# A decoder layer on one core: a new order and new lags for the attention stage, its norm factors on ScalarE, and the weights split later

## What is computed

```python
q, k, v = (x @ W.T for W in (Wq, Wk, Wv))             # 16 heads of 8
att = einsum('nqhd,nkhd->nhqk', q, k)                 # the heads of one token attend to each other
out = einsum('nhqk,nkhd->nqhd', softmax(att / sqrt(8)), v).reshape(N, S, D)
x = layernorm(x + out @ Wo.T + bo)
scores = einsum('bhsd,bhtd->bhst', xpos(x), xpos(ctx, downscale=True)) * decay_mask
x = layernorm(x + einsum('bhst,bhtd->bhsd', scores, ctx))       # retention, no softmax
w, chosen = top_k(x @ gate, 2)                        # 2 of 8 experts, softmax over the two
eo = einsum('ebsi,eih->ebsh', silu(x @ w1) * (x @ w3), w2)
x = layernorm(x + einsum('ebsh,bse->bsh', eo, tok_w))
# layernorm(x) = (x - mean) / sqrt(var + 1e-5), over the 128 features
```

## Time and profile before

| what | us |
|---|---|
| median of the three runs | 1015.34 |
| lowest and highest run | 1014.36, 1017.56 |
| the profiled execution, first to last instruction (span) | 1027.0 |
| first to last copy of q and v (ScalarE), 32 duos | 23.1 to 500.0 |
| first expert matmul | 652.3 |
| busy: TensorE, VectorE, ScalarE, GpSimd | 839.8, 794.7, 607.7, 654.8 |

### The profile page before, as it was taken

One profiled execution on the slowest core, in us unless ns is written; L12 is line 12 of the kernel. 1 busy time (PEld: TensorE's weight loads), 2 busy tenths in 40 slices (PEclk: granted clock), 3 DMA queues, 4 the chain that ended last, 5 costly groups with the idle time before them and its releaser, 6 DMA issues.

```text
span 1027.0 us, 35115 instructions
## 1 busy us (share of the span) xinstructions
PE 839.8 (82%) x12164; PEld 639.6 (62%) x12164; DVE 794.7 (77%) x2219; ACT 607.7 (59%) x1416; POOL 654.8 (64%) x738
## 2 busy tenths in 40 slices
PE   1667699999999999989979770699999999999600
PEld 1445466666666666656655440599899999999500
DVE  4787899998988989878856642588888888888575
ACT  1123457667667777666766851466666666666355
POOL 0338776699989999988997456044444444444443
PEclk9687899999999999999998965799999999999855
DMA  9312122122232231212222002222222222222186
GB/s 307 79 27 48 35 52 54 36 66 67 47 72 52 65 68 50 65 37 60 47 50 63 23 22 63 66 64 61 61 63 65 65 62 64 63 61 59 45 257 222
DMA packets 145303, 72.72 MB, mean 71 GB/s; under 512 B 75024, under 2 KB 134544, under 8 KB 145136
## 3 DMA queue, kind: packets, MB, share of 16 engines
q1 hardware_dynamic: 124800, 40.56, 17.1%
q0 software_dynamic: 8640, 17.84, 5.2%
q10 hardware_dynamic: 11696, 12.08, 3.6%
HBM read 42.11 MB, written 28.34 MB: 69 GB/s over the span
## 4 chain that ended last, share of the span: by engine, by line
PE 33%; POOL 28%; issue 11%; DVE 3%; DMA 2%; another core or an unknown queue 1%; ACT 1%; POOLq 0%; SPq 0%; DVEq 0%; ACTq 0%
POOL prod_ev L1551 14%; POOL routed_rows L1568 9%; PE QKV L773 9%; PE ST L773 9%; PE XT L801 5%; PE SC L801 5%; POOL rs L1531 3%; DMA prod_ev<-token_halves 1%; DMA routed_rows<-xe,pos 1%; PE YY L589 1%; POOL frs L1613 1%; PE YY L791 1%; PE TR L791 1%; PE SC L562 1%
## 5 line engine op out<-in xcount | busy, mean ns | idle before, releaser
L1551 POOL TENSOR_TENSOR prod_ev<-e_sb,q_v 128x512 f32<-128x512 f32 x256 | 300.3, 1206 | 77.5 <-PE YY L589 40.1
L1600 POOL DMA_INDIRECT token_halves<-w_new,tok_i x142 | 137.9, 971 | 32.5 <-issue 22.2
L1568 POOL DMA_INDIRECT routed_rows<-xe,pos x128 | 131.2, 1025 | 30.4 <-issue 30.0
L1151 DVE TENSOR_TENSOR prod_qk<-q_v,QKV 128x2048 f32<-128x2048 f32 x64 | 145.4, 2274 | 4.9 <-ACT q_v L870 4.9
L1453 DVE TENSOR_TENSOR prod_ev<-prod_qk,prod_ev 128x1024 f16<-128x1024 f32 x71 | 87.0, 1225 | 56.1 <-ACT prod_ev L1028 31.1
L773 PE MATMUL QKV<-k_t,w_hl 128*128 128x256 f16 x852 | 117.2, 274 | 0.0
L773 PE MATMUL ST<-k_t,w_hl 128*128 128x256 f16 x852 | 116.9, 274 | 0.0
L411 POOL TENSOR_TENSOR marks<-half_c 128x1 f32<-128x1 f32 x103 | 19.7, 192 | 149.7 <-DVE w_new L1469 149.1
L1037 ACT ACTIVATE prod_qk<-QKV,silu_scale 128x512 f32<-128x512 f32 x142 | 90.0, 683 | 41.3 <-PE QKV L773 41.3
L1028 ACT CAST prod_ev<-prod_qk 128x1024 f16<-128x1024 f32 x71 | 74.2, 1045 | 62.9 <-DVE prod_qk L1479 62.9
L1479 DVE SCALAR_TENSOR_TENSOR prod_qk<-ST,hid_scale,prod_qk 128x512 f32<-128x512 f32 x142 | 99.5, 742 | 2.9 <-PE ST L773 1.8
(11 more groups left out here) (171 smaller groups left out, 1785.9 us busy)
## 6 DMA issues: line engine op xcount, KB each, us to landing
w_new<-routed_rows SPq DMA_DIRECT2D x71, 130.0 KB
prod_ev<-token_halves SPq DMA_DIRECT2D x16, 512.0 KB, 4.9
x_sb<-x SPq DMA_DIRECT2D x32, 128.0 KB, 2.8
x_res<-x SPq DMA_DIRECT2D x128, 32.0 KB
head_rows<-o_n SPq DMA_DIRECT2D x32, 128.0 KB
o_t<-head_rows SPq DMA_DIRECT2D x64, 64.0 KB
ctx_sb<-ctx SPq DMA_DIRECT2D x32, 128.0 KB
out<-prod_qk ACTq DMA_DIRECT2D x16, 256.0 KB, 4.0
```

Of the source, the lines that this page charges most:

```text
L1151: eng.tensor_tensor(prod_qk[:, u, :, :].rearrange("p d (i j) -> p d i j", j=NH), q.unsqueeze(3).to_broadcast([P, HD, NH, NH]), k.unsqueeze ...
L1551: ins = eng.tensor_tensor(prod_ev[:, u, q, :, :, 0:HD], e_sb[:, it.slot(2), u, 64 * q:64 * q + 64].rearrange("p (i j) -> p j i", j=4).unsq ...
L1568: eng.indirect_dma_start(out=xs, out_offset=bass.IndirectOffsetOnAxis(ap=pos[:, r, 2 * u + k:2 * u + k + 1], axis=0), in_=xe[:, r, u, k, : ...
L1600: eng.indirect_dma_start(out=halves, out_offset=bass.IndirectOffsetOnAxis(ap=tok_i[:, s, u:u + 1], axis=0), in_=yw[:, s, u, :], in_offset= ...
```

## The change

- **Order and lags.** Each engine's `step` has a new order and new lags. The depth of the pipeline stays: from the projection to the last row numbers there are 13 steps in both. SyncE loads x at lag 0 and TensorE takes it at lag 6, so x is requested further ahead.
- **Norm factors.** `variances`, GpSimd's `one_over_std` and GpSimd's `norm_shift` go, and `NORM_GAP` with them. Each norm now has a logarithm and an exponential on ScalarE, exp(-0.5 ln(var + eps)), and a `norm_shift` on VectorE.
- **Transposes.** Keys and queries are transposed in TensorE's transpose mode, the two parts of each accumulating. The residual takes x from `x_t`, transposed back the same way, instead of a second load `x_res`; `x_t` gets a ring of 8.
- **DMA.** x comes in four pieces in the order of the heads, once a duo instead of twice; the heads are written in four pieces with the rows in place; they are read back one step after they were written.
- **Start.** The identity and the first x are requested first, then the rest; the weights follow the first x, two of them on SyncE's queue. The measuring and splitting of the weights stand in steps 8 to 13, where the first `products` stand in step 8.
- **Small.** `stand` goes; `one_hot` is one instruction instead of two; the third stage is unrolled (`C_FIRST`).

The diff, cut to its core (the waits that changed only their numbers are left out, and the removed text of `step`, which is printed above):

```diff
+X_RING = 8
-    PE_LAGS, ACT_LAGS, DVE_LAGS, POOL_LAGS, SP_LAGS = 13, 13, 14, 11, 9
-    NORM_GAP = 2
+    PE_LAGS, ACT_LAGS, DVE_LAGS, POOL_LAGS, SP_LAGS = 19, 20, 20, 21, 9
-    C_FIRST, C_LAGS = 8, 3
+    C_FIRST, C_LAGS = n_chunks_c, 3
-        x_t = sb("x_t", [2, 2, P])
+        x_t = sb("x_t", [X_RING, 2, P])
...
         def _(eng):                                        # sync
-            eng.dma_start(tab[:, :], table).then_inc(tab_in, 16)
+            def load_x(it):
+                wait(it, xt_done, RING)
+                for u in range(2):
+                    for b in range(2):
+                        eng.dma_start(x_sb[S * u:S * u + S, it.slot(RING), b, :], x_rows[it.number()][u][b]
+                                      ).then_inc(x_in[it.slot(RING)], 16)
+            def store_heads(it):
+                wait(it, on_ready)
+                wait(it, y_done, RING)
+                for u in range(2):
+                    for b in range(2):
+                        eng.dma_start(head_rows[it.slot(RING)][u][b],
+                                      o_n[S * u:S * u + S, it.slot(2), b, :, :].rearrange("p d h -> p (d h)")
+                                      ).then_inc(heads_out[it.slot(RING)], 16)
+            split = where["ident"][1]
+            eng.dma_start(tab[:, 0:split], table[:, 0:split]).then_inc(ident_in, 16)
+            load_x(Item(eng, None, None, 0))
+            eng.dma_start(w_qkv_sb[:, :], w_qkv).then_inc(qkv_in, 16)
+            eng.dma_start(tab[:, split:], table[:, split:]).then_inc(tab_in, 16)
...
             def step(at):
+                if (it := at(0)) and it.off > 0:
+                    load_x(it)
+                    if it.off == 3:
+                        load_weights(2)
+                        load_weights(1)
+                if it := at(9):
+                    load_context(it)
+                if it := at(7):
+                    load_heads(it)
+                if it := at(6):
+                    store_heads(it)
...
             def residual(it):                              # tensor
-                eng.matmul(Y, ones_bf[:, :], bo_bf[:, :], start=True, stop=False, skip_group_check=True)
+                for b in range(2):
+                    eng.matmul(Y[:, P * b:P * b + P],
+                               x_t[:, it.slot(X_RING), b, :], ident,
+                               is_transpose=True, start=(b == 0), stop=False, skip_group_check=True)
+                eng.matmul(Y, ones_bf[:, :], bo_bf[:, :], start=False, stop=False, skip_group_check=True)
-                    mm = eng.matmul(Y[:, P * b:P * b + P], ident, x_res[:, it.slot(RING), b, :], start=False, stop=True,
-                                    skip_group_check=True)
...
-                    eng.matmul(XKT[:, P * u:P * u + P], xk_a[:, u, :], ident, start=True, stop=False)
-                    mm = eng.matmul(XKT[:, P * u:P * u + P], xk_b[:, u, :], ident, start=False, stop=True)
+                    eng.matmul(XKT[:, P * u:P * u + P], xk_a[:, u, :], ident, is_transpose=True, start=True, stop=False)
+                    mm = eng.matmul(XKT[:, P * u:P * u + P], xk_b[:, u, :], ident, is_transpose=True, start=False, stop=True)
...
             def step(at):                                  # tensor; lags in brackets, in order
+                gates (19), queries_across (15), ret_scores 1 (16), scores 1 (9), residual (12), ret_values (16),
+                half_over (9), keys_across (15), own_heads (16), quarter_over (9), rows_across (18), project (7),
+                sums 0 (10), ret_scores 0 (15), ranks (19), tokens_across (6), scores 0 (8), sums 1 (10)
...
             eng.wait_ge(x_in[0], 64)                       # scalar
             eng.dma_start(fresh(0).rearrange("p (e i) -> p e i", e=n_exp), w1.rearrange("e h i -> h e i")).then_inc(w_in[0], 16)
+            def logarithm(it, norm):
+                s = it.slot(2)
+                wait(it, (mv1_ready, mv2_ready)[norm])
+                wait(it, rs_ready[norm], 2)
+                eng.activation(lnv[:, s, norm, :], mv[:, s, norm, :, 1], ACT.Ln, bias=eps_c[:, 0:1]).then_inc(ln_ready[norm], 1)
+            def one_over_std(it, norm):
+                s = it.slot(2)
+                wait(it, ln_ready[norm])
+                wait(it, nb_ready[norm], 2)
+                wait(it, (x1_ready, x2_ready)[norm], 2)
+                eng.activation(rs[:, s, norm, :], lnv[:, s, norm, :], ACT.Exp, scale=-0.5).then_inc(rs_ready[norm], 1)
             def step(at):                                  # scalar; lags in brackets, in order
+                blocks (16), row_ids (20), logarithm 0 (14), second_norm (18), queries_across (15), ret_across (16),
+                one_over_std 0 (14), logarithm 1 (17), beside 0 (10), beside 1 (10), other_over_own (19),
+                keys_across (15), one_over_std 1 (17), first_norm (14), exponent (9), rows_across (18),
+                residual (12), project (7), tokens_across (6), high_part 0, 1, 2 in steps 8, 10, 12
...
+            def norm_shift(it, norm):                      # vector
+                s = it.slot(2)
+                wait(it, rs_ready[norm])
+                wait(it, (x1_ready, x2_ready)[norm], 2)
+                eng.scalar_tensor_tensor(out=nb[:, s, norm, :], in0=mv[:, s, norm, :, 0], scalar=-1.0, in1=rs[:, s, norm, :],
+                                         op0=ALU.mult, op1=ALU.mult).then_inc(nb_ready[norm], 1)
-                for u in range(2):
-                    ins = eng.tensor_tensor(oh[:, s, u, :, :], twice(const("iota_e")),
-                                            ix8[:, s, u, 0:2].unsqueeze(2).to_broadcast([P, 2, n_exp]), ALU.is_equal)
+                eng.tensor_tensor(oh[:, s, :, :, :], twice(const("iota_e")).unsqueeze(1).to_broadcast([P, 2, 2, n_exp]),
+                                  ix8[:, s, :, 0:2].unsqueeze(3).to_broadcast([P, 2, 2, n_exp]), ALU.is_equal).then_inc(oh_ready, 1)
             def step(at):                                  # vector; lags in brackets, in order
+                queries_by_cos and sin (15), mask 0 (16), spread 2 (17), products 0 (8), logits (19), one_over (11),
+                places (20), top_values (19), counts (20), mask 1 (16), score_max (9), products 1 (8), max_of_two (9),
+                moments 2 (17), top_places (19), spread 1 (13), max_of_four (9), divide (11), chosen_places (20),
+                one_hot (19), positions (20), subtract_max (9), norm_shift 0 (14), second_residual (16), chosen (19),
+                moments 1 (13), keys_by_cos (14), gate_weights (19), keys_by_sin (14), norm_shift 1 (17),
+                measure 0, 1, 2 in steps 8, 9, 11; weight_scale in 8, 10, 12; low_part in 10, 12, 13
...
-            def one_over_std(c, d):                        # gpsimd
-                eng.tensor_tensor(rs[:, slot, :, :].rearrange("p k u -> p (k u)"),
-                                  ve[:, slot, :, :].rearrange("p k u -> p (k u)"), half_c[:, 0:4], ALU.pow).then_inc(rs_ready, 1)
-            def norm_shift(c, d):
             def step(at):                                  # gpsimd; lags in brackets, in order
+                weighted 0 second half (10), weighted 1 (10), scatter 1 (21), scatter 0 (20), weighted 0 first half (9)
```

More of the change, by code:

```diff
@@ new lines, in store_heads, with load_heads @@
+            def store_heads(it):
[6 more added lines that the diff above has]
+                                      ).then_inc(heads_out[it.slot(RING)], 16)
+            def load_heads(it):
+                r = it.slot(RING)
+                wait_ring(it, heads_out, per=64)
+                for u in range(2):
+                    eng.dma_start(o_t[:, r, u, :, :],
+                                  heads[r, u].rearrange("(g t) (d h) -> (t d) g h", t=NH, d=HD)).then_inc(y_in[r], 16)
@@ L468, in step @@
-                if it := at(HEADS_LAG):
-                    r = it.slot(RING)
-                    wait(it, y_done, RING)
-                    for u in range(2):
[L473 to L479, removed]
-                        eng.dma_start(o_t[:, r, u, :, :],
-                                      heads[r, u].rearrange("(g t) (d h) -> (t d) g h", t=NH, d=HD)).then_inc(y_in[r], 16)
+                if (it := at(0)) and it.off > 0:
[3 more added lines that the diff above has]
+                        load_weights(1)
@@ L1006, in step @@
-                weights(at)
+                if at_step(at, 1):
+                    blank_spare()
+                if it := at(16):
+                    blocks(it)
+                if it := at(20):
+                    row_ids(it)
+                if it := at(14):
+                    logarithm(it, 0)
+                if it := at(18):
+                    second_norm(it)
+                if it := at(15):
+                    queries_across(it)
+                if it := at(16):
+                    ret_across(it)
@@ new lines, in step @@
+                if it := at(14):
+                    one_over_std(it, 0)
```

(33 more changed lines are left out.)

537 lines of the change are left out of this document (234 added, 303 removed).

## The result

The changed kernel takes 1083.28 us (median of four runs, 1081.43 to 1086.72), the kernel before 1016.03 beside it (1014.36 to 1017.56). The ratio is 1.0643, with a 95% interval from 1.0602 to 1.0683: slower by 67 us, where 49 were forecast.

The account below looks back on a forecast made before the run. GpSimd was taken to bound the kernel before (15.74 us a step), ScalarE with table loads after; start -4, 24 steps +33, emptying +18, last 38 us +3, third stage -1 gave +49 on 1015.3: 1064 us (1035 to 1105).

Parts of the forecast that it names:

- the likeliest case: Whole kernel: ScalarE, with table loads between Ln and Exp, sets the step; 1035 to 1105 us, chance 0.76.
- Each need gets its own load: On ScalarE: Ln's set lacks Exp, so four passages a step each cost a 1.28 us load, about 128 more loads.
- ScalarE's sum: ScalarE a duo: 11.14 busy, 0.85 Ln and Exp, 5.13 loads, 0.36 lost overlaps, 17.5 us; with 0.2 waits, step 17.7.
- The step that failed: TensorE: not waited for at a step of 17.7 us, so halved transpose records, 1.7 us a duo at best, count nothing.
- The even part: 24 steps from duo 7's to duo 31's copy of q and v: 419.7 us instead of 386.4, +33.
- The base: Whole kernel: the span's 11.7 us over the median before carries over, so +49 is added to 1015.3.
- Emptying: From duo 31's copy to its first norm: four emptying steps of 15.2 us on ScalarE; 110 instead of 92, +18.
- The start: Up to duo 7's copy: x requested first, first copy at 16 instead of 23.1; net -4 us (-12 to +6).
- The heads: SyncE's write and read-back: heads arrive about 5.6 us into the next step, fitting by about 1.5 us.
- The first rival: ScalarE's tables: one set serves Ln and Exp, passages cost nothing, GpSimd sets a 14.3 us step; 959 us, chance 0.14.

Follow-up runs that it names:

- one-set kernel: The changed kernel with one table set for Ln, Exp, Identity and copies loaded once, ahead of ScalarE's first instruction; 945.38 us, ratio to before 0.9306.
- the experiment: The changed kernel, table loads and all, with TensorE doing the sums of half 0 two and a half times in a row; 1058.94 us, ratio 1.0440.
- The two experiments on the requests: Weights requested first, on top of the one-set kernel: two on SyncE's queue ahead of x, 963.88 us; all three on ScalarE's queue, 956.15 us.
- the power on GpSimd: The one-set kernel with the norm factor taken back to GpSimd, one power instruction of 128x2 for each norm; 981.53 us, ratio 0.9691.
- the last experiment: The one-set kernel with VectorE's chosen_places and positions (posw and its sum) moved from behind divide to behind second_residual; 950.26 us, ratio 0.9337.

## Why the prediction was right, and where its sum fell short

The forecast was 1064 us and the measured time 1083; the direction, the mechanism and the likeliest case were right.

- **Each need gets its own load.** The assumption on which all hung, Ln's set without Exp and four passages a step, is shown by the 128 loads: with no set named in the kernel's text, 64 stood ahead of the Lns and 64 ahead of the first Exp after each. A set with both functions exists and serves all of the first stage once the kernel's text names it, as the one-set kernel's two loads show.
- **ScalarE's sum** was 17.5 us a duo and 17.7 a step. With the clock held up the step is 17.1, the lower bound as stated, though its own terms (17.7 less 0.36 and 0.45) come to 16.9: Ln and Exp took 0.30 and 0.20 each for the 0.21 assumed, and the 0.56 given to waits and lost overlaps were not needed.
- **The step that failed** is "TensorE is not waited for at 17.7 us, so this counts nothing". It took TensorE's time from rows at a clock of 1.00. Once ScalarE set the pace, TensorE stood idle twice in each step with one group of sums between (0.9 and 2.1 us in its timeline), its granted clock fell to 0.87, and ScalarE then waited for slower transposes (438 ns for 290) and later values: 1.4 us a step, 24 us of the total by the experiment. The even part came out only 11 us above its forecast because ScalarE's sum erred the other way, by 0.6 us a step, some 13 us over the 21 full steps; that the two partly cancel is luck.
- **The base.** That the 11.7 us by which the profiled execution of before stood over its median would carry over was wrong. Of the 18 us that were missing (67 measured, 49 forecast) the spans show 9, and this is the other 9.
- **Emptying** was +21.9 for +18: steps of 15.0 to 15.9 between `rt` copies, 15.2 forecast. The clock was 0.67 there; what that cost was not tried by itself.
- **The start** came out at -6.3 for -4, with the first copy at 17.8 for 16. The two experiments on the requests bear out that x ahead of the weights brings it forward: 15.4 with one set, 32.8 and 25.7 with the weights first.
- **The heads** fit, as worked out: in 240 to 480 SyncE waited 154.3 us for `divide`, and TensorE's waits show none for `o_t`. With one set and steps of 14.1 they begin to show, 7.0 us in that window.
- **The first rival** was priced at 959; the kernel that is this rival takes 945. Its step in 240 to 480 and its emptying were right to 0.2 us and 0.5 us. But duo 7's copy came 5 us earlier than priced, the 24 steps took 336.7 us for 348, and the stretch to the last row count 28.9, 9 less than before where nothing was priced. The span is 29 us shorter than priced and the median 14; most of the difference is the 11.7 us of the base.

What stays open: if the parts add up, which was not tried, the one-set kernel's gain of 70 us is 36 of the norm factor, about 11 of the requests and some 23 of order, lags, transposes and the single load of x. These were not taken apart further, except that the transposes of keys and queries give nothing measurable.

## What to carry to other kernels

Before a function moves to ScalarE, list the functions in program order and count the passages between table sets: one line that names a set serving all of them was worth 138 us here, and grouping alike functions without it 81. Price a load by the slack of the step that it lands in, not by its own length: the same load cost 0.22 us in one kernel and 1.08 in the other. And when the bound moves to another engine, look again at what the engine that now waits does to its own clock: TensorE's was 0.87 here, where it had been 1.00.

## What the runs showed of the hardware

- Adding work to TensorE, 1.9 us a step of repeated products (3.13 us for the sums of half 0, 1.19 in the changed kernel), made the kernel 24 us faster: the granted clock of the even part rose from 0.87 to 1.00.
- Posw or one_hot, whichever came first, VectorE instructions of 128x32 with both inputs in SBUF, took 0.5 to 1.8 us and once 5.98 instead of 0.18 when it came up during GpSimd's products; with the power on GpSimd posw took 2.06 on average. Others that ran during the products kept their time: 2276 ns on average for the products of q and k, with one input in PSUM, with one set, 2282 in the changed kernel; and 161 for `FIND_INDEX8 ix<-mx,lg` of 128x8, 159 in the changed kernel. The latter's inputs are both in SBUF too, so the last experiment's theory went too far: two inputs in SBUF are not enough for the wait by themselves. What else it takes was not tried. Posw lasted past the ends of single products to the end of the row: from 474.85 to 480.83, with products of 1.17 us.
- GpSimd's power of 128x2 took 716 ns, of 128x4 1085 ns.
